# A fourth score bank and eight DMA semaphores in a causal attention and ternary feed-forward layer

## The chip, the cores and the metric

The kernel runs on one Trainium2 chip, on all 8 of its cores, with one program and one launch. Each core has its own two sequences, and no core waits for another. The metric is device time in microseconds (us) of the slowest core. The engines are called PE (TensorE), DVE (VectorE), ACT (ScalarE) and SP (SyncE, which here issues every DMA).

## What is computed

The reference is one transformer layer in float32 with 16 heads of 64, 16 sequences of 2048 tokens and width 1024. Cut to what matters:

```python
q = (x @ Wq).reshape(b, s, 16, 64)            # k, v alike
scores = einsum('bqhd,bkhd->bhqk', q, k) / 8
scores = scores - 50.0 * strict_upper_triangle # causal
out = einsum('bhqk,bkhd->bqhd', softmax(scores), v)
x = layernorm(x + out.reshape(b, s, 1024) @ Wr)
# feed-forward, INNER = 4096: ternary weights, 8-bit activations
gate = silu(bitlinear(x, w_gate)); up = bitlinear(x, w_up)
x = layernorm(x + bitlinear(gate * up, w_down))
```

`bitlinear` rounds its weights to -1, 0, 1 times a scale that is the mean absolute value of the whole matrix, and its activations to 8 bits per token.

## The kernel before

Each core goes through its two sequences one after the other (`run_seq`), with a barrier over all engines between the stages: transposing x, attention (8 pairs of heads, `attn_pair`), the output product with the first layer norm (`wr_ln1`), and the feed-forward (`ffn`). The program is written out by hand: `Plan.add` records each operation on its engine's list together with semaphore values to wait for, and every engine runs its list strictly in that order. The waits of all operations are made in line 83.

**Attention of a pair.** First q, k and v of the pair are projected (PE, banks 0 to 3), k and q are split into a high and a low bf16 half, and v is transposed in 128-column pieces (line 637) through banks 6 and 0 into `vp`. Then come 8 rounds, two heads by four query tiles `qt` of 512 queries. A round has n = 4, 8, 12 or 16 key blocks `kc` of 128 keys, for the causal half alone. It is called "the round of 4" and so on below, and its parts in the order of PE's list are:

- n score blocks (lines 661 to 672): two bf16 matmuls each, `bank<-klp,khl` and `bank<-qlo,khp`, into one PSUM bank. The first of them waits until the exponentials that last read this bank are done (`bank_user`). Before the change the banks are 0, 1 and 7 in rotation.
- two small matmuls into bank 5 (`bank<-rlb,ones_bf`, line 746) that spread the reciprocal row sums of the round before over 64 partitions.
- n value products (line 706), `bank<-abuf,vp`, float32, each two PE instructions, into one of the banks 2, 3, 4. Product kc waits for the exponentials of block kc.

ACT makes the exponentials of a block out of its bank into `abuf` (lines 679 to 696). The last four blocks of a round lie on the diagonal: there DVE first adds a mask in the bank (`bank<-bank,mask`, line 683), and ACT makes two instructions of all but the first of them.

DVE's list in a round is: the reciprocal of the last round's row sums and its split into `rlb` (`do_norm_pre`), three steps of weight preparation (`pump_prep(3)`), the four masks, the four operations that normalise the last round's output (`do_normalize`), and four more steps (`pump_prep(4)`).

**Weight preparation** runs inside the first sequence's attention only. Per weight matrix it has a first sweep of 32 steps, each with a `TENSOR_REDUCE` of a 128x1024 piece `pw` into `pacc`, one step for the scale, and a second sweep of 96 steps: three operations on a piece (`pterf`, `pterf`, `pter`), after the third of which SP issues a transposing DMA (`dmat`, `pterT<-pter`), a store (`wuT_sc<-pterT` and the like) and, at the next step, the load of a later piece. There are 3 matrices and 387 steps, seven in a round: about 14 rounds with the first sweep, 41 with the second and the last seven or eight with none.

**DMA semaphores.** `dma` takes its semaphore in rotation out of `NDMA`, and makes SP wait first until the DMA that last had this semaphore has landed:

```python
        sem = self.dma_sems[self._dma_rot]
        self._dma_rot = (self._dma_rot + 1) % self.NDMA
        w = list(waits) + [(sem, self.p.counts[sem])]
```

`dmat` waits for all of them, so a transposing DMA starts only when every DMA before it has landed, and nothing is issued on SP ahead of its turn. `Plan.emit` leaves out a wait whose value the engine has already waited for.

Of the kernel before, what the change touches and what calls it, by code (L numbers as in the profile page):

```python
# [96 lines left out]


class Builder:
    NDMA = 16  # L100

    def __init__(self, nc, cfg: CFG):
        self.nc, self.c = nc, cfg
        self.p = Plan(nc)
        self.dma_sems = [f"dma{i}" for i in range(self.NDMA)]
        for s in self.dma_sems + ["pe", "act", "dve"]:
# [29 lines left out]
    def dma(self, out_ap, in_ap, waits=()):  # L136
# [3 lines that stand above are left out]
# [5 lines left out]
    def dmat(self, out_ap, in_ap, waits=()):  # L145
        sem = self.dma_sems[self._dma_rot]
        self._dma_rot = (self._dma_rot + 1) % self.NDMA
        fence = [(ss, self.p.counts[ss]) for ss in self.dma_sems]
# [361 lines left out]
    def attn_pair(self, s, pair, XT_hi, XT_lo, wstage, nbufs):  # L510
        c = self.c
        S, D, DC, QT, KC = c.S, c.D, c.DC, c.QT, c.KC
        with ExitStack() as _es:
# [136 lines left out]
            for h in (0, 1):  # L650
                hi_q, lo_q = qk["q"]
                for qt in range(QT):
# [6 lines left out]
                        self.pump_prep(3)  # L659
                    t_exp = [None] * kc_hi  # L660
                    for kc in range(kc_hi):
                        bk = (0, 1, 7)[kc % 3]
                        w0 = [self.bank_user[bk], t_qk[-1], t_v[-1]] + \
                            self.t_qrep_done
                        t_s = self.mm(self.bank[bk],
                                      khl[h][:, kc * 128:(kc + 1) * 128],
                                      qrep[h][:, qt * 512:(qt + 1) * 512],
                                      True, False, waits=w0)
                        t_s = self.mm(self.bank[bk],
                                      khp[h][:, kc * 128:(kc + 1) * 128],  # L670
                                      lo_q[:, qt * 512:(qt + 1) * 512],
                                      False, True, waits=())
                        self.last_score_tok = t_s
                        a_off = kc * 128 - qt * 512
                        ab = abuf[:, kc * 512: kc * 512 + 512]
                        w_e = [t_s, self.ab_user.get(kc), t_vp_last]
                        t_el = []
                        if a_off + 128 <= 0:
                            t_el.append(self.act(ab, self.bank[bk], AF.Exp,
                                                 bias=self.negC, scale=0.125,  # L680
                                                 waits=w_e))
                        else:
                            t_m = self.tt(self.bank[bk][:, a_off:a_off + 128],
                                          self.bank[bk][:, a_off:a_off + 128],
                                          self.mask, ALU.add,
                                          waits=[t_s, self.t_consts[0]])
                            w_e = [t_m, self.ab_user.get(kc), t_vp_last]
                            if a_off > 0:
                                t_el.append(self.act(ab[:, 0:a_off],
                                                     self.bank[bk][:, 0:a_off],  # L690
                                                     AF.Exp, bias=self.negC50,
                                                     scale=0.125, waits=w_e))
                            t_el.append(self.act(ab[:, a_off:512],
                                                 self.bank[bk][:, a_off:512],
                                                 AF.Exp, bias=self.negC,
                                                 scale=0.125, waits=w_e))
                        self.bank_user[bk] = t_el[-1]
                        t_exp[kc] = t_el
# [577 lines left out]
```

How the kernel before makes its waits and increments, by code:

```python
                def body(eng):  # L77
                    last = {}
                    for emit, waits, inc, tag in plans.ops[eng_name]:
                        for s, v in waits:
                            if last.get(s, -1) >= v:
                                continue
                            eng.wait_ge(plans.sems[s], v)
                            last[s] = v
                        try:
                            instr = emit(eng) if emit is not None else None
                        except Exception:
                            print(f"EMIT FAILED at {tag} on {eng_name}")
                            raise
                        if inc is not None:
                            s, k = inc
                            instr.then_inc(plans.sems[s], k)
```

## Time and profile before

| | us |
|---|---|
| runs of the kernel | 7018.56 and 7502.58, median 7260.57 |
| the profiled execution | 7040.75 |
| span of its slowest core (core 3) | 7039.1 |
| spans of the eight cores | 6959.8 to 7039.1 |
| mean granted TensorE clock of core 3 | 0.855 of full speed |

The span runs from the first to the last instruction of the core; the 1.65 us between it and the execution's own time lie around it. In core 3's span the first sequence's rounds lie between 215.65 and 2260.33, the second sequence's between 3861.18 and 5622.64, each with the projections of the pairs in between.

### The profile page before, as it was taken

The numbers are of one execution on the slowest core, as the hardware profiler recorded it, in microseconds if no ns is written. First come the engines' busy times: TensorE is split into PE (matmuls) and PEld (weight loads), VectorE is DVE, ScalarE is ACT, GpSimd is POOL, SyncE is SP. The second block draws the span as 40 slices with busy tenths as digits, with TensorE's granted clock in tenths as the row PEclk, the third lists the DMA queues.
The fourth block names the chain that finished last, engine by engine and source line by source line (L and its number), as shares of the span: only waits on it lengthen the run. The fifth ranks groups of instructions, "written<-read, shape, count | busy, mean of one in ns | idle before, by whom it ended". The sixth has DMA issues, their size and how long they took to land.

```text
span 7039.1 us, 56723 instructions; the slowest of 8 cores (6959.8 to 7039.1 us)
## 1 busy us (share of the span) xinstructions
PE 5051.7 (72%) x17938; PEld 1861.1 (26%) x17938; DVE 2896.9 (41%) x4986; ACT 1123.8 (16%) x2132; POOL 0.2 (0%) x4
## 2 busy tenths in 40 slices
PE   2788778777777966565634888888888887557384
PEld 1222222222222432232212222222232233223131
DVE  3555655556544632241313444444444453223131
ACT  0212112112112111010100221122112211001010
POOL 0000000000000000000000000000000000000000
PEclk9688888888888988888877998898889998789797
DMA  4324324324221555555453000000000054544554
GB/s 111 114 69 107 103 77 115 80 86 127 68 61 35 137 132 162 139 142 161 132 167 72 12 18 15 19 12 18 16 19 11 7 159 129 155 129 146 139 151 141
DMA packets 802020, 649.78 MB, mean 92 GB/s; under 512 B 516800, under 2 KB 713664, under 8 KB 801728
## 3 DMA queue, kind: packets, MB, share of 16 engines
q1 hardware_dynamic: 801728, 646.16, 33.7%
q8 instruction: 151, 2.47, 0.1%
q14 instruction: 141, 1.16, 0.1%
HBM read 469.89 MB, written 75.50 MB: 77 GB/s over the span
## 4 chain that ended last, share of the span: by engine, by line
PE 57%; DMA 18%; DVE 14%; issue 5%; ACT 5%; SPq 1%; DVEq 0%; ACTq 0%
PE bank L160 56%; DMA wdsb<-wdT_sc 7%; ACT abuf L171 4%; DVE rls L209 3%; DMA hqT<-hq 3%; DMA wgsb<-wgT_sc 1%; DMA pterT<-pter 1%; SPq L143 1%; DVE pacc L204 1%; DVE vp L198 1%; DMA XqT<-xqtm 1%; DMA XT_lo<-xlo 1%; DMA x_tm<-x 1%; PE bank L166 1%; DMA z2b<-y_sc 1%
## 5 line engine op out<-in xcount | busy, mean ns | idle before, releaser
L171 ACT ACTIVATE abuf<-bank,negC 128x512 f32<-128x512 f32 (+3 forms) x1664 | 829.8, 602 | 2945.1 <-DVE bank L188 2122.9
L160 PE MATMUL bank<-abuf,vp 128*65 128x512 f32 x2560 | 1275.8, 658 | 0.0
L160 PE MATMUL bank<-wdsb,hqT 128*128 128x512 bf16 x2048 | 546.5, 419 | 665.2 <-DMA wdsb<-wdT_sc 665.1
L160 PE MATMUL bank<-klp,khl 128*128 128x512 bf16 x1280 | 507.4, 396 | 402.1 <-ACT abuf L171 379.5
L160 PE MATMUL bank<-XT_hi,apwh 128*128 128x512 bf16 x1536 | 427.0, 441 | 479.0 <-DVE apwl L193 479.0
L160 PE MATMUL bank<-wgsb,XqT 128*128 128x512 bf16 x2048 | 496.8, 386 | 249.0 <-DMA wgsb<-wgT_sc 247.5
L209 DVE RECIPROCAL rls<-bank 1x512 f32<-1x512 f32 x128 | 429.5, 3355 | 551.7 <-PE bank L160 550.9
L160 PEld LDWEIGHTS bank<-abuf,vp 128*65 128x65 f32 x2560 | 377.4, 152 | 858.4 <-issue 858.4
L160 PE MATMUL bank<-qlo,khp 128*128 128x512 bf16 x1280 | 512.1, 400 | 0.0
L160 PE MATMUL bank<-wusb,XqT 128*128 128x512 bf16 x2048 | 487.9, 381 | 0.0
L160 PEld LDWEIGHTS bank<-wdsb,hqT 128*128 128x128 bf16 x2048 | 201.6, 105 | 1008.7 <-issue 855.2
L188 DVE TENSOR_TENSOR htsb<-bank,gts 128x512 f32<-128x512 f32 x256 | 177.0, 691 | 665.8 <-PE bank L160 604.7
L193 DVE SCALAR_TENSOR_TENSOR z2a<-bank,cdc,z2a 128x512 f32<-128x512 f32 x32 | 22.8, 749 | 902.7 <-PE bank L160 902.7
L160 PEld LDWEIGHTS bank<-XT_hi,apwh 128*128 128x128 bf16 x1536 | 166.7, 110 | 734.1 <-issue 613.3
L160 PEld LDWEIGHTS bank<-klp,khl 128*128 128x128 bf16 x1280 | 125.6, 98 | 888.0 <-issue 862.5
L160 PE MATMUL bank<-XT_hi,apwl 128*128 128x512 bf16 x1536 | 350.1, 381 | 0.0
L160 PE MATMUL bank<-XT_lo,apwh 128*128 128x512 bf16 x1536 | 349.5, 381 | 0.0
L160 PEld LDWEIGHTS bank<-wgsb,XqT 128*128 128x128 bf16 x2048 | 201.9, 99 | 501.8 <-issue 269.1
L171 ACT ACTIVATE gts<-bank,cg_cols 128x512 f32<-128x512 f32 x256 | 175.9, 687 | 682.2 <-PE bank L160 682.1
L160 PEld LDWEIGHTS bank<-wusb,XqT 128*128 128x128 bf16 x2048 | 201.6, 98 | 247.1 <-issue 9.5
L188 DVE TENSOR_TENSOR bank<-bank,mask 128x128 f32<-128x128 f32 x512 | 137.2, 296 | 229.7 <-PE bank L160 224.5
L198 DVE CAST qhi<-bank 128x512 bf16<-128x512 f32 x64 | 43.9, 686 | 385.7 <-PE bank L160 385.7
(90 smaller groups left out, 3451.5 us busy)
## 6 DMA issues: line engine op xcount, KB each, us to landing
wdsb<-wdT_sc SPq DMA_DIRECT2D x256, 512.0 KB, 3.8
wgsb<-wgT_sc SPq DMA_DIRECT2D x64, 1024.0 KB, 8.9
wusb<-wuT_sc SPq DMA_DIRECT2D x64, 1024.0 KB, 11.3
pw<-Wg SPq DMA_DIRECT2D x64, 512.0 KB, 4.7
pw<-Wu SPq DMA_DIRECT2D x64, 512.0 KB, 4.4
pw<-Wd SPq DMA_DIRECT2D x64, 512.0 KB, 5.0
x_tm<-x SPq DMA_DIRECT2D x8, 2048.0 KB, 17.9
xrd<-x SPq DMA_DIRECT2D x32, 512.0 KB, 5.4
```

Of the source, the lines that this page charges most:

```text
L143: e.dma_start(out=o, in_=i), w, (sem, 16))
L160: e.matmul(o, l, r, start=a, stop=b),
L166: e.transpose(o, i, d), waits, ("pe", 1))
L171: e.activation(o, i, f, bias=b, scale=s, accum_out=a),
L188: e.tensor_tensor(o, a, b, p), waits, ("dve", 1))
L193: e.scalar_tensor_tensor(o, a, s, b, p0, p1, accum_out=ac),
L198: lambda e, o=out_ap, i=in_ap: e.tensor_copy(o, i),
L204: e.tensor_reduce(o, i, AX, p, apply_absolute_value=a),
L209: lambda e, o=out_ap, i=in_ap: e.reciprocal(o, i),
```

## The change

Scores rotate over four banks, 0, 1, 6 and 7, in place of 0, 1 and 7, and DMAs rotate over 8 semaphores in place of 16. Bank 6 was used by the transposes of v at the head of each pair and by `wr_ln1`, and by nothing during the rounds.

```diff
 class Builder:
-    NDMA = 16
+    NDMA = 8
...
                     for kc in range(kc_hi):
-                        bk = (0, 1, 7)[kc % 3]
+                        bk = (0, 1, 6, 7)[kc % 4]
                         w0 = [self.bank_user[bk], t_qk[-1], t_v[-1]] + \
                             self.t_qrep_done
```

No instruction is added, taken away or moved on any engine; banks and waits change. On PE, in the second round of the first pair (a round of 8), with the numbers of the banks and the semaphores that each row waits for, the rows before are:

```order
L160 MATMUL bank7<-klp0,khl0 128x512 [waits sem_act]
L160 MATMUL bank7<-qlo,khp0 128x512
L160 MATMUL bank0<-klp0,khl0 128x512 [waits sem_act]
L160 MATMUL bank0<-qlo,khp0 128x512
L160 MATMUL bank1<-klp0,khl0 128x512 [waits sem_act]
L160 MATMUL bank1<-qlo,khp0 128x512
L160 MATMUL bank5<-rlb,ones_bf 64x512 [waits sem_dve]
L160 MATMUL bank5<-rlb,ones_bf 64x512
L160 MATMUL bank4<-abuf,vp0 65x512 x5
L160 MATMUL bank4<-abuf,vp0 65x512 [waits sem_act] x3
```

and in the changed kernel:

```order
L160 MATMUL bank6<-klp0,khl0 128x512 [waits sem_act]
L160 MATMUL bank6<-qlo,khp0 128x512
L160 MATMUL bank7<-klp0,khl0 128x512 [waits sem_act]
L160 MATMUL bank7<-qlo,khp0 128x512
L160 MATMUL bank5<-rlb,ones_bf 64x512 [waits sem_dve]
L160 MATMUL bank5<-rlb,ones_bf 64x512
L160 MATMUL bank4<-abuf,vp0 65x512 x4
L160 MATMUL bank4<-abuf,vp0 65x512 [waits sem_act] x4
```

The last score block waited for the exponentials of the fifth, so that five value products needed no wait of their own; now it waits for those of the fourth.

On SP, in the second block of 512 tokens of the first sequence's feed-forward, where the down weights are loaded, the rows before are:

```order
L143 DMA wdsb<-wdT_sc 128x2048 [waits sem_pe,sem_dma12]
L143 DMA wdsb<-wdT_sc 128x2048 [waits sem_pe] x13
L143 DMA y<-z2a 128x1024 [waits sem_dve]
L143 DMA y<-z2b 128x1024 [waits sem_dve]
```

and in the changed kernel:

```order
L143 DMA wdsb<-wdT_sc 128x2048 [waits sem_pe,sem_dma4]
L143 DMA wdsb<-wdT_sc 128x2048 [waits sem_pe] x7
L143 DMA wdsb<-wdT_sc 128x2048 [waits sem_pe,sem_dma5]
L143 DMA wdsb<-wdT_sc 128x2048 [waits sem_pe,sem_dma6]
L143 DMA wdsb<-wdT_sc 128x2048 [waits sem_pe,sem_dma7]
L143 DMA wdsb<-wdT_sc 128x2048 [waits sem_pe,sem_dma0]
L143 DMA wdsb<-wdT_sc 128x2048 [waits sem_pe,sem_dma1]
L143 DMA wdsb<-wdT_sc 128x2048 [waits sem_pe,sem_dma2]
L143 DMA y<-z2a 128x1024 [waits sem_dve,sem_dma3]
L143 DMA y<-z2b 128x1024 [waits sem_dve,sem_dma4]
```

The fence of a transposing DMA covers the next 8 DMAs in place of the next 16, so more loads have a semaphore wait of their own. Of the 256 down loads, 72 had one before and 156 have one now.

## Rows read from the trace of the kernel before

**Rows 1.** The page: the span, and the chain that ended last.

```profile
span 7039.1 us, 56723 instructions; the slowest of 8 cores (6959.8 to 7039.1 us)
...
PE 57%; DMA 18%; DVE 14%; issue 5%; ACT 5%; SPq 1%; DVEq 0%; ACTq 0%
```

**Rows 2.** Waits, whole span: who waited for whom, us in total, times, longest.

```profile
PE bank L160 <- ACT abuf L171: 379.5, 127, 12.7
```

**Rows 3.** Windows, one head's rounds, second sequence: span, busy by engine, clock, DMA share.

```profile
4622.08:4635.40 13.32, 8.46 (x19) 2.29 (x18) 7.91 (x11) 2.98 (x7) 0.00 (x0) 0.74 0.04 10
4635.40:4649.65 14.25, 11.77 (x36) 3.49 (x35) 7.92 (x11) 5.29 (x11) 0.00 (x0) 1.00 0.04 10
4649.65:4667.40 17.75, 17.51 (x51) 5.10 (x50) 8.12 (x11) 7.61 (x15) 0.00 (x0) 1.00 0.03 8
4667.40:4690.90 23.50, 23.26 (x67) 6.72 (x66) 9.95 (x13) 10.02 (x19) 0.00 (x0) 1.00 0.10 28
```

**Rows 4.** Timeline of PE, the round of 4 at 4622: start, us, operation, idle before.

```profile
4628.39 0.59 PE L160 MATMUL bank<-klp,khl 128*128 128x512 bf16 x1 [4.86 <-ACT abuf L171]
...
4630.32 5.24 PE L160 MATMUL bank<-abuf,vp 128*65 128x512 f32 x8
```

**Rows 5.** The same round: DVE's last `rlb` operation, and the chain's first exponential.

```profile
4626.40 0.68 DVE L193 SCALAR_TENSOR_TENSOR rlb<-rls,rlb 1x512 bf16<-1x512 f32 x1
...
4627.56 0.70 ACT abuf L171
```

**Rows 6.** Timeline of the round of 8 at 4635, all engines.

```profile
4636.09 2.42 ACT L171 ACTIVATE abuf<-bank,negC 128x512 f32<-128x512 f32 x4 [5.29 <-PE bank L160]
...
4639.72 0.68 DVE L193 SCALAR_TENSOR_TENSOR rlb<-rls,rlb 1x512 bf16<-1x512 f32 x1
...
4641.66 0.38 PE L160 MATMUL bank<-klp,khl 128*128 128x512 bf16 x1 [2.41 <-ACT abuf L171]
...
4642.18 0.61 PE L160 MATMUL bank<-rlb,ones_bf 1*64 1x512 bf16 x2
```

**Rows 7.** The chain in a round of 12: exponentials of blocks 8 and 9, last score.

```profile
4585.52 0.73 ACT abuf L171
4586.33 0.70 ACT abuf L171
...
4587.16 12.03 PE bank L160 x30
```

**Rows 8.** Windows: first sequence's heads and pairs; last, a round of 8, second sequence.

```profile
842.83:939.65 96.82, 67.93 (x170) 19.06 (x169) 72.90 (x105) 26.02 (x52) 0.00 (x0) 0.81 0.46 158
...
1122.63:1204.78 82.15, 67.33 (x170) 18.97 (x169) 52.95 (x74) 25.91 (x52) 0.00 (x0) 0.85 0.53 125
...
1041.94:1204.78 162.84, 133.21 (x337) 37.60 (x338) 98.52 (x142) 52.15 (x104) 0.00 (x0) 0.85 0.49 118
...
1850.56:2024.45 173.89, 139.33 (x337) 38.78 (x338) 103.28 (x146) 51.83 (x104) 0.00 (x0) 0.82 0.51 112
...
3939.28:3955.50 16.22, 13.46 (x36) 3.87 (x35) 7.91 (x11) 5.29 (x11) 0.00 (x0) 0.89 0.04 10
```

**Rows 9.** Timeline of SP, second sweep: transposing DMAs and the load between two.

```profile
1141.38 1.25 SPq L150 DMA_TRANSPOSE pterT<-pter  x1
...
1145.23 0.64 SPq L143 DMA_DIRECT2D pw<-Wu  x1
1149.48 1.22 SPq L150 DMA_TRANSPOSE pterT<-pter  x1
...
1191.69 1.53 SPq L150 DMA_TRANSPOSE pterT<-pter  x1
```

**Rows 10.** Timeline of DVE, first sweep: a reduction; the next begins at 255.42.

```profile
253.83 1.22 DVE L204 TENSOR_REDUCE pacc<-pw 128x1 f32<-128x1024 f32 x1
```

**Rows 11.** The densest run of DMAs: the first's landing (chain), the ninth's issue (SP).

```profile
2733.36 8.15 DMA wgsb<-wgT_sc
...
2746.42 4.62 SPq L143 DMA_DIRECT2D z2b<-y_sc  x2
```

## The prediction

> **What bounds the kernel now.** I read the page first: the chain that ended last is 57% PE, and the execution took 7040.75 us, 1.65 us more than its slowest core's span [rows 1]. The two runs shown lie on both sides (7018.56 and 7502.58, median 7260.57); the sum below is made against 7040.75, near the lower one, and says nothing of a disturbed run. Then the waits: 127 times PE waits for an exponential, 379.5 us in all [rows 2], almost exactly once in each of the 128 rounds. Then the windows of single rounds and the timelines inside them, which tell what that wait is. In the second sequence a head's four rounds take 13.3, 14.3, 17.8 and 23.5 us [rows 3]. In the rounds of 12 and 16 PE is busy for all but 0.24 us by the profile, but scores come at ACT's pace there; in the rounds of 4 and 8 PE stands still for 4.9 and 2.4 us ahead of the last score block [rows 4, 6]. With three banks the last score block n-1 needs the exponential of block n-4, the first diagonal one, and that needs its mask on DVE, which stands behind the reciprocal. So the value products, whose own inputs are long ready, queue on PE behind one score block that waits for DVE. With four banks the last block needs block n-5: not on the diagonal, no mask. In the round of 4 it needs nothing.
>
> **The change part by part, second sequence.** What PE waits for next is `rlb` on DVE, then value product kc's own exponential.
>
> Round of 4: before, the first exponential ends at 4627.56 + 0.70 = 4628.26 [rows 5], and then the last score, the two bank-5 matmuls and only then the products follow, from 4630.32 [rows 4]. Now score 4 has gone out at once, the bank-5 matmuls run from the end of `rlb`, 4626.40 + 0.68 = 4627.08, and the products can start with the first exponential, at about 4628.4: 1.9 us sooner. The clock eats part of it. The eight product instructions took 5.24 us [rows 4], 0.65 each, because the round's granted clock was 0.74 on average: a stretch at 1.2 GHz after the long idle [rows 3]. If that stretch ends when it did, products that start earlier run more of their time in it, and 1.2 us of 1.9 are left. I take 1.2; the ends are 0 (all of it lost to the low clock) and 3.6 (no fall at all: products from 4628.4 at 0.86 us each, the last held by its exponential, done about 4631.7 against 4635.4).
>
> Round of 8: exponentials 0 to 3 are done at 4636.09 + 2.42 = 4638.51, so the last score goes out near 4639. `rlb` is ready at 4639.72 + 0.68 = 4640.40, so the bank-5 matmuls start at about 4640.5 in place of 4642.18 [rows 6]: 1.7 us. The products of blocks 4 to 7 start 3.4 us later than the first and find their exponentials done. Four of the second sequence's 16 such rounds took 16.2 us at a clock of 0.89 [rows 8] where the others took 14.3; with the idle shortened I expect most of them to keep 2.4 GHz: 0.5 us per round. Together 2.2, from 1.7 to 2.2.
>
> Rounds of 12 and 16: the last score leaves 0.14 us after the second of two neighbouring exponentials (4586.33 + 0.70 to 4587.16), and now leaves after the first (4585.52 + 0.73) [rows 7]: 0.8 us each. `rlb`, about 5 us after the round's start, is ready by then.
>
> A head: 1.2 + 2.2 + 0.8 + 0.8 = 5.0 us; 16 heads: **80 us** (60 to 118). The first sequence's last seven rounds have no weight preparation: **9 us**.
>
> **First sequence.** Here DVE has seven preparation steps in each round, and the mask came behind three of them: PE stood still longer and there is more to win on PE, but DVE and the DMA queue become late next.
>
> First sweep, 14 rounds. DVE's list takes about 4.7 us for reciprocal and `rlb`, seven steps of 255.42 - 253.83 = 1.59 [rows 10] = 11.1, masks 1.2 and normalising 2.7: 19.7 us. A head took 96.8 us [rows 8]. Without the wait for the mask, three of its rounds are held by DVE and the last by PE at 23.5 - 0.8 = 22.7: 3 x 19.7 + 22.7 = 82, some 15 less; I take 13 for the loads that DVE still waits for: 3.5 heads, **45 us** (20 to 60).
>
> Second sweep, 41 rounds, 5.1 pairs. DVE's list is shorter (steps of some 0.8 us), and PE alone could bring a head from 82.2 us [rows 8] to about 68, as now in the second sequence. But the DMAs do not let it. A transposing DMA waits for everything in flight, and the next load follows it: load at 1145.23, next transpose at 1149.48; from 1141.38 to 1191.69 there are 6 periods of 8.4 us [rows 9], and SP is never ahead. A round wants 7/3 of them, 19.6 us, against 82.2 / 4 = 20.5 now. What is left comes from the ends: the queue runs empty during the projections, and a late mask costs nothing in a round of 12 or 16 once products of 8 or 12 earlier blocks stand ahead of it. So: 16 periods of 8.5 from the first transpose (5 us into the pair) to the last that the last round needs (14 us into it) put that round's start at 136 + 5 - 14 = 127 and the pair's end at 127 + 22.7 = 150, against 162.8; with the slower period of the last matrix (9.1) 160 against 173.9 [rows 8]. That is 13 a pair; I take 10, since where two third steps fall into one group of four, DVE is held ahead of the next reciprocal. 5.1 pairs: **50 us** (10 to 100).
>
> **Eight semaphores.** At the densest place the first of a run of DMAs has landed 8.15 us after 2733.36 and the ninth is issued at 2746.42 [rows 11], 4.9 us later; no DMA of the trace was issued before the eighth ahead of it had landed. So the wait never holds SP; it is one more semaphore instruction. 84 more down loads have one on a path that PE waits for. Successive issues lie 0.05 to 0.1 us apart, DMA issue aside, and I bound the wait by that from above and by nothing from below: 0 to 8 us, **3 us** taken. If the cover went (a landing 5 us longer), z2b loads would slip that are needed some 100 us later.
>
> Sum: 7040.75 - 80 - 9 - 45 - 50 + 3 = 6859.75, so **6860 us**. The likeliest case's own range is 6800 to 6920.
>
> **Rivals.**
>
> The clock holds in the rounds of 4. The idle before the first product shrinks and is cut in two by the bank-5 matmuls. For it: rounds of 8 with 2.4 us of idle mostly kept 1.00 [rows 3, 6]. Against it: about 3 us of idle remain in one piece, and 1.2 GHz followed 4.9. It would give 3.6 - 1.2 = 2.4 us more in each of 32 rounds: 77, so 6860 - 77 = 6783.
>
> The preparation takes everything back in the first sequence. For it: SP's transposes are back to back now [rows 9]. Against it: the first sweep has none. Then only the 89 us remain: 7040.75 - 89 + 3 = 6955, within 2%.
>
> The change does not do what it says, because something else holds the last score or bank 6. Against it: PE's order shows the last score waiting for ACT alone, and bank 6 is free in the rounds. About 7043.
>
> Slower: the low clock spreads. Place: the rounds of 12 and 16, at 1.00 now [rows 3]. If PE, done with its scores a block sooner, idled before `rlb` and each of these 64 rounds got a stretch at 1.2 GHz like the round of 4's, a product would cost 1.71 in place of 0.86 us; with four products in it that is 3.4 us a round, 218 in all: 6860 + 218 = 7078. It decides from about 2.8 us a round (181 / 64). Against it: in these rounds `rlb` is ready before the last score. Beside it, by the Trainium skill, page "TensorE: Matmul & The Clock Gate", section "A second HAM failure mode: psum-queue depth-cycling", bf16 matmuls that cycle through PSUM banks idle briefly so often that the clock swings between its levels, which speaks for this rival. By that rule the rounds of 12 should swing already; the trace has 1.00 there with three banks in rotation, so it does not agree, and by the trace the term stays nothing.
>
> **How the numbers follow.** Forecast 0.50, clock holds 0.22, preparation takes it back 0.21, no effect 0.04, slower 0.03. The range goes from 6750 (the clock case with a little of the second sweep's upper end) to 6970 (the take-back case with the eight semaphores at their dearest and its rounds of 4 at less than 1.2); outside are the last two cases and the tails. A measurement of this kernel tells about 2%, 141 us, from no change. Faster by more: 0.50 + 0.22 + 0.01, with a little of the forecast's low tail given away to "same": 0.73. Slower: 0.03. Same: 0.24.
>
> **What would show it.** In the changed profile: rounds of the second sequence near 12.1, 12.5, 17.0 and 22.7 us; PE's wait for exponentials ahead of a last score gone and a wait for `rlb` of about a microsecond in rounds of 8 in its place; DVE's waits for `pterT<-pter` well over the few now in the first sequence, with transposes still 8 to 9 us apart; feed-forward stages as long as before. Wrong if rounds of 4 run at a clock of 1.00 (too little forecast), if pairs of the second sweep stay at 163 us or fall under 145, or if SP waits for a landed DMA eight back.

## The result and the profile after

| | before | changed |
|---|---|---|
| runs measured together | 10, median 7178.38 us, lowest 6997.16 | 13, median 7074.31 us, lowest 6850.99 |
| ratio, time over time before | | 0.9802, 95% interval 0.974 to 0.9864 |

In many runs of either kernel, eight of the changed one's 13, the cores of one die or both had a lower granted clock for a time and the run was some per cent longer; the ratio leaves such runs out, and the readings of profiles below leave out such cores for that time. The changed kernel is 0.98 of the time before: on 7040.75 us that is 139 us less, with an interval from 96 to 183. Whether it is faster by more than the 2% that counts as told from no change, the runs don't decide. The forecast, 6860 us, is a ratio of 0.974, just at the interval's end. The median of all 13 runs, 7074, lies outside its range of 6750 to 6970, since the sum was made against the one execution of 7040.75 us; the five runs behind the ratio took 6850.99, 6866.09, 6882.15, 6884.77 and 6918.15. Two more executions, outside the table, took 6851.63 and 7075.82.

In the profiled execution core 3, of die 0, is compared with core 3 of before (7039.1 us). Its span and clock, and those of the two dies:

```profile
core 3: 6867.5 us, clock 0.861
...
die 0 (median of its cores): 6854.0 us, clock 0.859
die 1 (median of its cores): 7030.9 us, clock 0.824
```

What a reader should look at first is the wait that the change was to take away. The waits of core 3 (who waited for whom: us in total, times, longest):

```profile
PE bank L160 <- DMA wdsb<-wdT_sc: 669.6, 209, 26.3
...
PE bank L160 <- DVE apwl L193: 489.3, 37, 123.9
...
PE bank L160 <- DVE rlb L193: 235.2, 79, 10.6
...
DVE pter L178 <- DMA pterT<-pter: 199.4, 70, 7.7
...
PE bank L160 <- ACT abuf L171: 53.0, 23, 5.3
```

PE's wait for exponentials fell from 379.5 us in 127 places [rows 2] to 53.0 in 23. Two others grew: PE's for `rlb` was 10.0 us in 2 places before (235.2 in 79 now), and DVE's for a transposing DMA was 77.8 us in 29 (199.4 in 70 now). So 326 us of waiting went and 347 us came on two engines, and the time fell by some 170 on this core. Sums of waits don't add up to time; the place of each does.

The windows of core 3, the first four being one head of the second sequence as in [rows 3], the fifth another round of 8, then the whole of the second sequence's rounds and the two pairs of [rows 8]:

```profile
4501.55:4513.02 11.47, 7.63 (x20) 2.34 (x18) 7.82 (x11) 2.88 (x7) 0.00 (x0) 0.85 0.05 11
4513.02:4527.30 14.28, 12.98 (x36) 4.06 (x34) 7.82 (x11) 5.30 (x11) 0.00 (x0) 0.88 0.04 9
4527.30:4544.29 16.99, 16.99 (x52) 5.30 (x50) 8.02 (x11) 7.61 (x15) 0.00 (x0) 1.00 0.04 9
4544.29:4567.03 22.74, 22.74 (x68) 6.92 (x67) 9.95 (x13) 9.82 (x19) 0.00 (x0) 1.00 0.10 29
4449.24:4461.82 12.58, 11.28 (x35) 3.68 (x34) 7.82 (x11) 5.30 (x11) 0.00 (x0) 1.00 0.05 12
3773.54:5464.75 1691.21, 1486.93 (x4814) 522.27 (x4814) 775.74 (x1257) 411.06 (x833) 0.00 (x0) 0.90 0.06 15
992.10:1147.82 155.72, 129.17 (x337) 38.86 (x338) 97.56 (x142) 51.77 (x104) 0.00 (x0) 0.87 0.50 119
1769.73:1939.81 170.08, 134.80 (x337) 40.10 (x338) 102.43 (x146) 51.44 (x104) 0.00 (x0) 0.83 0.53 115
```

Rounds of 12 and 16 fell from 17.75 and 23.50 us to 16.99 and 22.74, and PE is busy for all of them. The round of 8 comes in two kinds, 12.58 us at a clock of 1.00 and 14.28 at 0.88, about half and half. The two pairs gained 7.1 and 3.8 us, against the 13 and 14 worked out and 10 taken. They are the fourth and the seventh of the first sequence; the second, the only other with the second sweep in all its rounds, gained 18.4 (169.55 to 151.11), so that the three together come to 9.8 a pair. What the wait became is seen in PE's timeline of the first two windows:

```profile
4503.06 0.38 PE L160 MATMUL bank<-qlo,khp 128*128 128x512 bf16 x1
4506.70 0.59 PE L160 MATMUL bank<-rlb,ones_bf 1*64 1x512 bf16 x2 [3.26 <-DVE rlb L193]
4507.87 5.32 PE L160 MATMUL bank<-abuf,vp 128*65 128x512 f32 x8 [0.58 <-ACT abuf L171]
...
4516.49 0.38 PE L160 MATMUL bank<-qlo,khp 128*128 128x512 bf16 x1
4518.17 0.59 PE L160 MATMUL bank<-rlb,ones_bf 1*64 1x512 bf16 x2 [1.30 <-DVE rlb L193]
4518.68 8.78 PE L160 MATMUL bank<-abuf,vp 128*65 128x512 f32 x16
```

The fourth score goes out at once and is no longer the one that waits. PE then stands 3.3 us before `rlb` in the round of 4, where it stood 4.9 before the last score [rows 4], and 1.3 us in the round of 8, where it stood 2.4 [rows 6]. In this round of 8 a value product's instruction takes 8.78 / 16 = 0.55 us: the clock was down for a part of it.

By stages, sums over PE's rounds, each the mean over cores (us). A first-sweep round is one in which the preparation's first sweep runs, and so on; the very first round, which has no steps, is counted with the first sweep, and where the border rounds between the sweeps are counted moves up to some 10 us from one row to the other:

| | before, 8 cores | after, cores 0 to 3 | difference | forecast |
|---|---|---|---|---|
| second sequence, rounds and projections | 1758.9 | 1691.3 | -68 | -80 |
| last 7 rounds of the first, no preparation | 127.5 | 117.9 | -10 | -9 |
| 15 first-sweep rounds | 360 | 322 | -38 | -45 |
| 42 second-sweep rounds | 889 | 834 | -55 | -50 |
| projections of the first sequence | 661 | 684.5 | +24 | 0 |
| all other stages | | | +6 | +3 |

The last row is what is left of the difference of the spans, 7000 to 6859 on average. The four gains together are 171 us where 184 were forecast. The row that nobody asked for is the projections of the first sequence.

### The profile page after: what moved, and what is told of

Its sections match the earlier page's. It is cut to its first block, busy times and chain, and to the rows that moved or that the text cites. A ratio compares the mean times of both kernels' runs of the same rounds, so it can differ in the third digit from the quotient of the medians.

```text
span 7071.7 us, 56292 instructions; the slowest of 8 cores (6821.6 to 7071.7 us)
## 1 busy us (share of the span) xinstructions
PE 5184.6 (73%) x17688; PEld 1944.3 (27%) x17938; DVE 2887.4 (41%) x4986; ACT 1113.3 (16%) x2132; POOL 0.2 (0%) x4
## 4 chain that ended last, share of the span: by engine, by line
PE 58%; DMA 22%; DVE 12%; issue 3%; SPq 2%; ACT 1%; DVEq 0%; ACTq 0%
PE bank L160 58%; DMA wdsb<-wdT_sc 7%; DMA hqT<-hq 3%; DMA pterT<-pter 3%; DVE rls L209 3%; SPq L143 2%; DMA pw<-Wu 1%; DMA otl_sc<-ogl 1%; DMA pw<-Wd 1%; DMA wusb<-wuT_sc 1%; DVE vp L198 1%; DMA x_tm<-x 1%; DMA XqT<-xqtm 1%; DMA XT_lo<-xlo 1%; DMA pw<-Wg 1%
## 5 line engine op out<-in xcount | busy, mean ns | idle before, releaser
L160 PE MATMUL bank<-abuf,vp 128*65 128x512 f32 x2560 | 1303.8, 671 | 50.1 <-ACT abuf L171 49.0
L160 PE MATMUL bank<-wgsb,XqT 128*128 128x512 bf16 x2010 | 540.8, 415 | 248.8 <-DMA wgsb<-wgT_sc 200.5
L160 PE MATMUL bank<-wusb,XqT 128*128 128x512 bf16 x2004 | 534.8, 412 | 12.3 <-DMA wusb<-wuT_sc 9.1
L160 PE MATMUL bank<-klp,khl 128*128 128x512 bf16 x1184 | 477.5, 403 | 0.0
L193 DVE SCALAR_TENSOR_TENSOR z2a<-bank,cdc,z2a 128x512 f32<-128x512 f32 x32 | 22.8, 749 | 871.9 <-PE bank L160 871.9
L160 PE MATMUL bank<-XT_hi,apwl 128*128 128x512 bf16 x1536 | 365.4, 393 | 0.0
L160 PE MATMUL bank<-XT_lo,apwh 128*128 128x512 bf16 x1536 | 365.4, 393 | 0.0
L160 PE MATMUL bank<-rlb,ones_bf 1*64 1x512 bf16 x256 | 95.6, 460 | 232.4 <-DVE rlb L193 232.3
L160 PEld LDWEIGHTS bank<-XT_hi,apwl 128*128 128x128 bf16 x1536 | 154.4, 101 | 195.0 <-issue 59.1
```

Source lines behind the costliest of these rows:

```text
L160: e.matmul(o, l, r, start=a, stop=b),
L193: e.scalar_tensor_tensor(o, a, s, b, p0, p1, accum_out=ac),
```

## Experiments

Each kernel is the one before with the edit shown. A single time is that of the profiled execution.

### The two edits apart

`e1_bank_only`:

```diff
-                        bk = (0, 1, 7)[kc % 3]
+                        bk = (0, 1, 6, 7)[kc % 4]
```

> The fourth score bank alone, with 16 semaphores as before. My theory: the whole difference is the bank, so this runs like the changed kernel: about 0.98 of the time before; rounds of the second sequence near 11.3, 13.4, 17.0 and 22.8 us on average (before 12.9, 14.8, 17.8, 23.6), the first sequence's projections some 24 us longer in all than before. Rival (the eight semaphores take part of the bank's gain back): 0.975 or less, with shorter feed-forward stages or shorter first-sequence projections than in the changed kernel.

Measured: 6860.97 us in the profiled execution, without a ratio (six more runs took 7033.43 to 7313.79 us); spans 6801.2 to 6859.4, mean 6828 against 7000 before. The kernel before took 7013.95 to 7081.23 us, 7033 on average, in twelve comparable runs beside it, so this one execution is at 0.976 of it, between the theory's 0.98 and the rival's 0.975. By stages: second sequence 1687.6, last seven rounds 118.6, first sweep 318, second sweep 824, projections of the first sequence 677. Its chain that ended last, by engine:

```profile
PE 58%; DMA 23%; DVE 13%; issue 3%; SPq 2%; ACT 1%; DVEq 0%; ACTq 0%
```

Every gain, and projections 16 us longer, are there with the bank alone. ACT's share of the chain fell from 5% [rows 1] to 1%, DMA's rose from 18% to 23%: the exponentials are off the path and the transfers came onto it.

`e2_sems_only`:

```diff
-    NDMA = 16
+    NDMA = 8
```

> Eight semaphores alone, with three score banks. My theory: no difference, 1.000 within 0.3%, every stage as before within 5 us, at most 8 us more in the two feed-forward stages. Rival: SP is held and it is slower by 20 us or more, which would show as longer feed-forward stages or projections.

Measured: ratio 1.0017, 95% interval 0.9991 to 1.0044, the same: a cost of 12 us with an interval from -6 to 31. The second sequence's attention took 1758.5 to 1762.0 us by core, as before (1757.9 to 1761.5). In the changed kernel SP's queue at the place of [rows 11] reads:

```profile
2633.50 0.55 SPq L143 DMA_DIRECT2D wgsb<-wgT_sc  x1
2634.13 0.83 SPq L143 DMA_DIRECT2D wusb<-wuT_sc  x1
2635.06 2.65 SPq L143 DMA_DIRECT2D wgsb<-wgT_sc  x1
2637.80 4.20 SPq L143 DMA_DIRECT2D wusb<-wuT_sc  x1
2642.15 3.73 SPq L143 DMA_DIRECT2D wdsb<-wdT_sc  x2
2646.03 0.79 SPq L143 DMA_DIRECT2D z2a<-y_sc  x2
2646.98 2.00 SPq L143 DMA_DIRECT2D z2b<-y_sc  x2
```

The ninth of the run goes out 13.5 us after the first, where it was 13.1 before: no stall.

### Why the projections of the first sequence grew

DVE and SP at a pair's end show a candidate. In the changed kernel, DVE (start, us, operation, idle before), in a last round of 16 that begins at 604.66 and ends at 627.56:

```profile
622.10 0.69 DVE L178 TENSOR_SCALAR pter<-pterf 128x1024 bf16<-128x1024 f32 x1 [2.31 <-DMA pterT<-pter]
622.90 0.75 DVE L182 TENSOR_SCALAR pterf<-pw,pgcol 128x1024 f32<-128x1024 f32 x1
624.11 0.69 DVE L182 TENSOR_SCALAR pterf<-pterf 128x1024 f32<-128x1024 f32 x1 [0.46 <-DVE pterf L182]
632.02 0.69 DVE L178 TENSOR_SCALAR pter<-pterf 128x1024 bf16<-128x1024 f32 x1 [7.22 <-DMA pterT<-pter]
632.63 0.69 DVE L198 CAST apwh<-wstage 128x1024 bf16<-128x1024 f32 x1
633.42 1.23 DVE L193 SCALAR_TENSOR_TENSOR apwl<-wstage,apwh 128x1024 bf16<-128x1024 f32 x1
```

and SP there:

```profile
618.88 1.24 SPq L150 DMA_TRANSPOSE pterT<-pter  x1
...
622.68 0.64 SPq L143 DMA_DIRECT2D pw<-Wg  x1
...
628.84 1.23 SPq L150 DMA_TRANSPOSE pterT<-pter  x1
```

For contrast, DVE at the end of the same pair in the kernel before, whose last round ends at 668.35:

```profile
657.50 0.68 DVE L178 TENSOR_SCALAR pter<-pterf 128x1024 bf16<-128x1024 f32 x1
658.28 0.75 DVE L182 TENSOR_SCALAR pterf<-pw,pgcol 128x1024 f32<-128x1024 f32 x1
659.14 0.69 DVE L182 TENSOR_SCALAR pterf<-pterf 128x1024 f32<-128x1024 f32 x1
663.52 0.69 DVE L178 TENSOR_SCALAR pter<-pterf 128x1024 bf16<-128x1024 f32 x1 [3.69 <-DMA pterT<-pter]
664.13 0.69 DVE L198 CAST apwh<-wstage 128x1024 bf16<-128x1024 f32 x1
664.92 1.22 DVE L193 SCALAR_TENSOR_TENSOR apwl<-wstage,apwh 128x1024 bf16<-128x1024 f32 x1
```

There DVE waited for a transpose too, but the next pair's weight copies `apwh` and `apwl` were done 2.2 us before the pair's end. With the rounds shorter and the transposes hardly quicker, the last step stands on DVE until the transpose before it has landed, 7.2 us, and `apwh` stands behind that step: it comes 5.1 us after the pair's end, and `apwl` is done 7.1 us after it. In the projections that follow PE waits 22.3 us for `apwl` in 3 places, against 15.1 in 2 before, and the next pair's first score is 101.4 us after the pair's end, against 93.3. This is the pair with the greatest lag: at the seven such places the projections of core 3 grew by 14 us in all, 8 of them here. Whether the bank or the preparation makes the projections longer, two kernels tell that run no preparation in the attention (it then all runs after it, so that the total is longer):

`e3_noprep_3`, and `e4_noprep_4` with the edit of `e1_bank_only` besides:

```diff
                     if self.norm_pending is not None:
                         self.norm_pending[0]()
-                        self.pump_prep(3)
...
-                    self.pump_prep(4)
```

> Three banks, no weight preparation inside the rounds: all of it runs after the first sequence's attention, so the whole is slower by several hundred us. Both theories: the first sequence's rounds take what the second's take before the change (12.9, 14.8, 17.8, 23.6 us on average, 1100 us for 64). It is the base for the next kernel.

> Four banks, no weight preparation inside the rounds. My theory (the preparation's DMA chain and DVE steps take back gain, partly by running into the next pair's projections): the first sequence's rounds shrink by about 75 us against the kernel with three banks, its projections do not grow (under 5 us), so about 70 us net, as in the second sequence. Rival (the longer projections come from the bank, since v's transposes share bank 6 with the scores): projections grow by some 24 us here too.

Measured: 7703.9 and 7581.02 us. The first sequence's attention took 1758.6 us on average with three banks, just the second sequence's time, and 1692.6 with four; the projections 660 and 659. The window of the first sequence's attention on core 3, three banks:

```profile
208.90:1967.48 1758.58, 1503.37 (x4814) 508.31 (x4814) 781.09 (x1257) 414.69 (x833) 0.00 (x0) 0.90 0.06 15
```

and four:

```profile
211.38:1906.07 1694.69, 1488.65 (x4814) 522.72 (x4814) 776.32 (x1257) 411.32 (x833) 0.00 (x0) 0.90 0.06 15
```

So the bank alone is worth 66 us in a sequence's attention, and the projections grow only where the preparation runs. What e4 leaves open is whether it is this step at a pair's end. The next kernel, which was run twice, takes the four steps out of a pair's last round (they come later); both with the fourth bank:

```diff
+                    self.last_round = h == 1 and qt == QT - 1
...
-                    self.pump_prep(4)
+                    self.pump_prep(0 if self.last_round else 4)
```

> Four banks, 16 semaphores, and the four preparation steps of each pair's last round left to later rounds. My theory (those steps wait for a transpose and hold the copies that the next pair's first projection needs): the first sequence's projections come back from 676 to 660 us; its last rounds, which had no steps, get some and take 10 to 20 us more, so the whole stays within 0.3% of the fourth bank alone. Rival (the projections grow because of the bank): they stay at 675 or more.

> Four banks, the four steps of each pair's last round moved to later rounds, once more. My theory: the first sequence's projections come back from 676 to about 660 us. Rival: 670 or more.

Measured, the first time: 7288.44 us, at a granted clock of 0.74 to 0.84 over the first sequence's attention on every core, where e1 had 0.85 to 0.87; it is not read further. The second time: 7153.66 us. On cores 0 to 3 the projections took 660, 658, 655 and 658 us, which is the time before. So the steps at a pair's end are the cause of what the bank added there. But nothing was won: the second sweep's rounds took 848 us in place of 824 (e1), the last seven 129 to 135 in place of 119, the attention 1947 to 1971 in place of 1938 (the expectation had 10 to 20 us more in the last rounds and nothing lost in all). Steps that don't stand at a pair's end stand elsewhere, as long as the chain of DMAs sets their pace.

### The chain of DMAs in the second sweep

Load, transpose and store follow each other because a transpose waits for all. These kernels leave out 29 of a matrix's 32 second-sweep loads (so a part of the weights is prepared from other pieces than theirs); where an expectation counts 93 of 96, it is these. `e5_noload_3` has three banks, `e6_noload_4` and its repetition have four:

```diff
                         if idx + 3 < n2:
-                            issue2(idx + 3)
+                            t_lds2[idx + 3] = None
```

> The same loads left out, with three banks. My theory: with three banks the rounds are held by the mask behind DVE's steps more than by the transposes, so the 41 rounds fall by 30 us or less from the 885 to 890 of before, and the fourth bank is then worth over 90 us in them in place of 50. Rival (DVE's list): no change with either number of banks, and the bank is worth 50 us here too.

> Four banks; the preparation's second sweep loads no later piece but its first three (93 of 96 loads per matrix side left out in all, the weights come out wrong), so that a transposing DMA waits for a store and no load. My theory (transposes back to back hold the first sequence's second-sweep rounds): their period falls from 8.5 to about 6.5 us and these 41 rounds take 760 us or less where the changed kernel takes 834 on core 3, and the first sequence's projections fall back from about 685 to 660. Rival (DVE's own list holds them): 820 or more, projections still over 675.

> Four banks, second sweep without the loads after the first three pieces of each matrix (29 of 32 per matrix left out, the prepared weights come out wrong), once more. With three banks the same cut took 12 us off the 41 second-sweep rounds (886 to 874). My theory (back-to-back transposes hold them once the bank no longer does): with four banks these rounds fall from about 824 to under 790 us and the first sequence's projections from 676 to about 660. Rival (DVE's own list): 812 or more, projections over 670.

Measured: with three banks the second-sweep rounds took 874 us, 15 less than with loads. `e6_noload_4` took 7235.73 us at a granted clock of 0.79 to 0.80 on every core, where e1 had 0.86 to 0.87, and is not read further; its repetition took 6789.22, and its second-sweep rounds 751 to 756 us by core, some 71 less than e1's 824. The first sequence's projections took 669 us, half of the way back from 677 to the 661 of before. The fourth bank is worth 889 - 824 = 65 us in the second-sweep rounds with the loads and 874 - 753 = 121 without. The mean time from one transpose to the next, gaps over 12 us left out, was 8.83 us before, 8.62 in e1 and 7.16 here. A pair without loads on core 3, against 155.6 us in e1:

```profile
958.64:1096.06 137.42, 122.29 (x337) 37.56 (x338) 97.62 (x142) 51.77 (x104) 0.00 (x0) 0.91 0.39 79
```

So the chain of DMAs takes back about half of what the bank gives there, and it did not bind much before.

`e13_load_first_plain` shortens the chain and leaves nothing out: the load that stood behind the transpose's store goes ahead of it, one piece earlier (four banks besides):

```diff
-                for idx in range(min(3, n2)):
+                for idx in range(min(4, n2)):
                     issue2(idx)
...
-                        if idx + 3 < n2:
-                            issue2(idx + 3)
...
                         t_ter_free = t_tr
+                        if idx + 4 < n2:
+                            issue2(idx + 4)
```

> Four banks, 16 semaphores; in the second sweep the load of a later piece is issued right after the transposing DMA and ahead of the store, and four pieces are loaded in place of three at its start; nothing is left out. My theory (a transposing DMA waits for the load that was issued last): the load starts 0.6 us sooner, the period falls from about 8.5 to 7.9 us, and the 41 second-sweep rounds with their projections take 15 to 35 us less than the 824 + 676 us of the fourth bank alone. Rival (the transposes are not what holds them): within 8 us.

Measured: ratio 0.9712, 0.9654 to 0.9769; its runs 6829.05 to 6853.17 us. On cores 2 to 5, whose clock in the first sequence's attention was 0.86 to 0.87 as in e1: second-sweep rounds 808 to 814 us, some 15 less than e1, projections 674, 3 less, attention 1916 to 1926, 19 less. The period went from 8.62 to 8.41 us, a third of the expected fall: the right direction, mis-sized.

### The clock in the rounds of 4 and 8

`e7_filler_mm` (four banks besides) puts matmuls whose result is overwritten where PE waits for `rlb`:

```diff
                     if self.norm_pending is not None:
+                        for _ in range({4: 13, 8: 5}.get(kc_hi, 0)):
+                            self.mm(self.bank[5][0:64, :],
+                                    self.ones_bf[:, 0:64],
+                                    khp[h][:, 0:512], True, True,
+                                    waits=[self.bank_user[5]], inc=False)
                         self.norm_pending[1]()
```

> Four banks, 16 semaphores, and idle PE time filled: 13 matmuls into bank 5 ahead of the bank-5 matmuls in rounds of 4, 5 in rounds of 8, whose results are overwritten. My theory (what is missing in the second sequence is a stretch at 1.2 GHz after idle time): rounds of 4 at a clock near 1.00 and under 10.8 us (now 11.0 to 11.3), rounds of 8 all at 12.6 (now 13.5 on average), the second sequence's attention 15 to 35 us shorter than 1688. Rival (the clock falls for another reason than idle time, or the fillers only lengthen the round): rounds of 8 still at 13.4 on average, or longer.

Measured: ratio 0.9714, 0.9678 to 0.975; its runs 6818.24 and 6824.52 us. The second sequence took 1651.1 us, 37 less than e1. Rounds of 4 and 8 on core 3:

```profile
4476.16:4485.93 9.77, 8.86 (x33) 3.28 (x31) 7.82 (x11) 2.88 (x7) 0.00 (x0) 1.00 0.00 0
4485.93:4498.51 12.58, 12.48 (x40) 4.15 (x39) 7.82 (x11) 5.30 (x11) 0.00 (x0) 1.00 0.09 22
```

PE did more work and was done sooner. All rounds of 8 are now of the kind of 12.58 us. Of the rounds of 4 only the second of each pair is like the one shown, 9.77 us at 1.00; the first of a pair, which follows the projections, took 10.8 to 11.2 us at a clock near 0.8 (the sequence's very first 7.5), so the average is 10.2 us at 0.89 and not the 1.00 expected. Against e1 a round of 8 gained 1.0 us and a round of 4 0.8 on average, 30 us in the sequence; the other 6 came in its projections (657 to 650 us).

### DVE ahead of the masks

What stands ahead of the diagonal masks on DVE, the reciprocal and three steps, made PE's wait. Two kernels put it behind them, with four banks (`e8_mask_first_4`) and with three (`e9_mask_first_3`): the reciprocal and `rlb` follow the masks, and the normalisation comes one round later.

```diff
-                    if self.norm_pending is not None:
-                        self.norm_pending[0]()
-                        self.pump_prep(3)
...
+                    if self.rest_pending is not None:
+                        self.rest_pending()
+                        self.rest_pending = None
                     if self.norm_pending is not None:
-                        self.norm_pending[1]()
+                        self.norm_pending[0]()
+                        self.rest_pending = self.norm_pending[1]
                         self.norm_pending = None
+                        self.pump_prep(3)
...
+            if self.rest_pending is not None:
+                self.rest_pending()
+                self.rest_pending = None
```

> Four banks, and DVE's list turned: masks of a round first, then the normalising of the round before the last, then the last round's reciprocal, the bank-5 matmuls a round later. My theory (rounds of 4 and 8 are held by the mask and by rlb, both behind the reciprocal): in the second sequence rounds of 4 near 7.5 us and of 8 near 11.2, its attention 80 to 110 us shorter than 1688; in the first sequence less, since the transposes hold it: 0 to 50 us. The whole 6720 to 6780 us, ratio 0.955 to 0.965. Rival (the order on DVE does not matter, ACT's pace does): second sequence within 15 us of 1688.

> The same with three banks. My theory: without DVE ahead of the mask, a last score block waits only for one exponential more, 0.7 to 0.8 us in rounds of 8, 12 and 16 and little in rounds of 4, so that the fourth bank is worth 35 to 45 us in the second sequence in place of 71. Rival (the fourth bank's worth does not depend on DVE's order): 65 us or more.

Measured: with four banks 6840.49 to 6857.62 us in four runs, without a ratio, where 6720 to 6780 was expected; with three banks 6958.69 and three runs from 7222.06 to 7392.49 us, without a ratio. Rounds of 4 and 8 on core 3, four banks:

```profile
4468.62:4474.47 5.85, 5.85 (x19) 1.94 (x18) 4.10 (x9) 2.87 (x7) 0.00 (x0) 1.00 0.00 1
4474.47:4486.28 11.81, 11.29 (x36) 3.69 (x35) 10.81 (x13) 5.29 (x11) 0.00 (x0) 1.00 0.09 22
```

and its wait at the head of a pair:

```profile
PE bank L161 <- DVE apwl L194: 614.5, 48, 125.1
```

The rounds of 4 and 8 came out near what was expected, 7.5 and 11.2 (the four kinds took 6.6, 11.8, 17.0 and 22.8 us on average), but the second sequence gained 46 us over e1, not 80 to 110: its projections grew from 656 to 710 us, because the normalisation of the last round but one now stands at the pair's end: its two bank-5 matmuls come behind the last value products on PE, DVE waits for them, and `apwh` and `apwl` stand behind it on DVE (PE's wait for them 614.5 us against 490.7 in e1). It is the lateness of the change once more, from another cause. In the first sequence, where steps stand behind the normalisation too, `apwl` was done 15 to 22 us after a pair's end on core 3: the projections took 804 to 817 us by core against e1's 677, which ate all that the rounds gained, and the attention 1956 against 1938. That, and the second sequence's projections, is why the whole missed its expectation. With three banks and masks first (cores 2, 3, 6 and 7, whose clock in the second sequence was 0.94) rounds of 4 to 16 took 7.1, 13.2, 17.8 and 23.6 us and the second sequence 1683: the fourth bank is worth 41 us there against 71 behind the reciprocal.

### A version that takes both

`e11_mid_flush` is `e8_mask_first_4` with the normalisation of the last round but one done between the value products of a pair's last round, without preparation steps, in place of the pair's end:

```diff
+                        if h == 1 and qt == QT - 1 and kc == 12:
+                            self.no_steps = True
+                            self.rest_pending()
+                            self.rest_pending = None
+                            self.no_steps = False
...
-            if self.rest_pending is not None:
-                self.rest_pending()
-                self.rest_pending = None
...
-                    self.pump_prep(4)
+                    self.pump_prep(0 if self.no_steps else 4)
```

and `e12_load_first` adds the edit of `e13_load_first_plain`.

> Four banks, masks first on DVE as before, but in a pair's last round the round before it is normalised after the twelfth value product, without steps, in place of behind them all. My theory (the 54 us more in the second sequence's projections came from DVE normalising at the pair's end, ahead of the copies that the next projection needs): those projections come back from 710 to 656 to 665 us, and the second sequence's attention takes 1590 to 1600. The whole 6740 to 6800 us. Rival (they came from the last reciprocal, which stands ahead of the transposes of v in either version): still over 700.

> The last two edits together. My theory: the gains add, 6710 to 6780 us, and this is the fastest version: ratio under 0.965. Rival: in the first sequence the turned order is held so much by the steps that nothing is added to the 6760 of the filler version.

Measured: e11 6752.9, 6763.0 and 6853.29 us, ratio 0.9639, 0.9449 to 0.983, so that alone it is not told from the 2%; e12 6734.77 and 6742.7, ratio 0.9567, 0.949 to 0.9644, the fastest of all. In e11 the second sequence took 1598.7 us with its projections at 661:

```profile
3740.34:5339.30 1598.96, 1435.99 (x4814) 510.78 (x4814) 785.78 (x1257) 410.15 (x833) 0.00 (x0) 0.94 0.06 16
4434.85:4440.70 5.85, 5.85 (x20) 1.93 (x19) 4.10 (x9) 2.87 (x7) 0.00 (x0) 1.00 0.00 0
4440.70:4452.51 11.81, 11.28 (x36) 3.66 (x35) 10.81 (x13) 5.29 (x11) 0.00 (x0) 1.00 0.09 23
```

The clock is 0.94 over the whole, where it was 0.90 with the change alone. e12's cores:

```profile
die 0 (median of its cores): 6693.6 us, clock 0.877
die 1 (median of its cores): 6702.1 us, clock 0.876
```

## Why the prediction was right or wrong

**What bounds.** Right. The last score's wait was the one to take away, and e3 and e4 show the bank's worth with no preparation beside it: 66 us in one sequence's attention, less than the 80 of the sum. (The range of 60 to 118 for it does not follow from its own ends, which give (0 + 1.7 + 0.8 + 0.8) x 16 = 53 from below.)

**Round of 4 (forecast 1.2 us).** 12.9 to 11.3 us on average, 1.6. The products start where the sum put them, and the clock fell as supposed. The rival in which the clock holds did not come; e7 shows what it would have been: 9.77 us in the rounds where fillers kept the clock at 1.00, and the prediction's 3.6 us less than 13.32 is 9.7.

**Round of 8 (forecast 2.2 us).** 14.8 to 13.4, 1.4. The failed words are "with the idle shortened I expect most of them to keep 2.4 GHz: 0.5 us per round". The wait for `rlb` came as said (1.3 us), the clock did not hold: half of these rounds ran at 0.88 where about three quarters ran at 1.00 before. e7 removed the idle and brought all to 12.58. Of the 12 us missing from the 80 this is 16 x 0.8 = 13; the rounds of 4 gave 6 more than forecast, the projections of the second sequence took 4 more, and the rest is rounding.

**Rounds of 12 and 16 (forecast 0.8 each).** 0.8 and 0.8. The rival of the spreading clock, by which these rounds would slow, did not come: 1.00 in both. By the Trainium skill ("TensorE: Matmul & The Clock Gate", "A second HAM failure mode: psum-queue depth-cycling") a kernel that cycles through PSUM banks idles so often between its matmuls that the clock swings. The trace does not agree for the rounds of 12 and 16: four banks in rotation run at 1.00 there. In the rounds of 8 it was the wait ahead of `rlb` that took the clock down, as e7 shows.

**First sweep (45) and second sweep (50).** 38 and 55 on cores 0 to 3, 42 and 65 in e1. Both lie within their bounds, and e5 and e6b confirm what was said to hold the second back: without loads the bank gives 121 us there. The working by pairs is right only on average: 13 and 14 us were worked out for two pairs that gained 7.1 and 3.8, and a third gained 18.4.

**Projections of the first sequence (nothing).** This is the step that failed. "What is left comes from the ends: the queue runs empty during the projections" supposed that the lag of the DMA chain is worked off behind the pair's end for nothing, "the pair's end at 127 + 22.7 = 150". PE's rounds do end sooner; but DVE is not done, and the next pair's first weights are copied behind the step that waits. It cost 16 us in e1. The 24 in the changed kernel are more than this step: cores 0 and 1, with 690 us each, had a clock of 0.845 in the first sequence's attention where e1's cores had 0.85 to 0.87, while cores 4 and 5, at 0.86 in that stage, had 679. e10b put the projections back to 658 and paid in the rounds. A shorter chain helped the rounds (e13, e6b) and brought the projections to 674 and 669; no run here removed the lag.

**Eight semaphores (3).** Not told from nothing: 12 us with an interval from -6 to 31. The changed kernel's cores 0 to 3 were some 30 us longer than e1's, 20 of them in the first sequence's attention and 4 in the second's, but this is not shown to be the semaphores. Cores 4 and 5 of the same execution, at a clock of 0.86 in the first sequence's attention, took 1937 and 1934 us for it, and e1 1938. And in the execution of 6851.63 us, at clocks of 0.864 to 0.867, the eight cores' spans are 6825 us on average, where e1's are 6828.

**The sum.** 181 us were forecast. By the mean spans 141 came on cores 0 to 3 (7000 to 6859) and 172 in e1; by the ratio 139. Of the 40 missing on cores 0 to 3, 24 are the projections of the first sequence and 12 the second sequence, the rounds of 8 above all. In e1 the same two terms missed by 16 and 9, and the second sweep gave 15 more than taken: that e1's total lies so near the forecast is in part luck. The changed kernel's best executions, 6851 us, lie there too.

## What to carry to other kernels

When an in-order engine waits for one late input ahead of work that is ready, one more buffer can move the wait to a block that is early, and it pays in the size of the gap to the next-latest input, here `rlb`. The same saving shortens the stage under everything that keeps its own pace beside it: look for what then arrives late at the stage's end, and what is queued behind it on its engine. Work that was deferred to fill a gap should be flushed before the next stage's first operation of the same engine: e11 does so, and the second sequence's projections went from 710 to 661 us.

## What the runs showed of the hardware

- An idle of 3.3 us in one piece in the round of 4 and 1.3 us in the round of 8 that follows left half of the rounds of 8 at a clock of 0.88, while before the change 4.9 and then 2.4 us left about three quarters of them at 1.00. Less idle did not mean a higher clock. Why is open; e7 shows that with this idle filled all of them run at 1.00.
- Matmuls that compute nothing needed are worth running: 18 to each head's rounds of 4 and 8 made the second sequence's attention 37 us shorter (1688 to 1651).
- 84 more waits of SP on a semaphore that had long been reached could not be measured (ratio 1.0017).
- A transposing DMA that waits for everything in flight came every 8.6 us on average with a load beside it (e1), every 8.4 with the load issued ahead of the store (e13) and every 7.2 without (e6b).
